# Gated cross attention with a routed expert layer: least and greatest of the last group read from the rows before normalization, routing choices of the first batches two steps earlier

## The reference

```python
x = x + tanh(g_xattn) * attention(layernorm(x), ctx)      # 16 heads of 16, rotary, causal, keys from ctx
xf = layernorm(x)                                          # (3584, 256)
stats = [mean, std, min, max, l2, share of |xf| < 1e-6]    # 6 per token
h = gelu(concat(xf, stats) @ r1_w.T + r1_b)                # 128 hidden
probs = softmax(h @ r2_w.T)                                # 32 experts, top 2 per token
# each expert keeps its 140 best tokens; expert and adapter outputs are added back
x = x + tanh(g_ffn) * out
```

## Time and profile before

| what | us |
|---|---|
| median of 3 runs | 772.27 |
| the runs | 772.27, 768.41, 773.79 |
| the profiled execution | 769.41 |
| its span, first to last instruction | 767.6 |
| busy TensorE, VectorE, ScalarE, GpSimd | 672.7, 526.5, 405.5, 322.6 |
| mean granted TensorE clock | 0.947 |

### The profile page before, as it was taken

The page is one execution under the profiler, slowest core; times in us unless marked ns, Lnnn a source line. Parts: engine busy times, 40 slices in busy tenths (PEclk is TensorE's granted clock), DMA queues, the critical chain, the costliest instruction groups (busy, mean ns, idle before and its releaser), DMA issues.

```text
span 767.6 us, 17452 instructions
## 1 busy us (share of the span) xinstructions
PE 672.7 (88%) x5247; PEld 528.0 (69%) x5247; DVE 526.5 (69%) x1548; ACT 405.5 (53%) x1569; POOL 322.6 (42%) x339
## 2 busy tenths in 40 slices
PE   8799999999999999999888212699999999999992
PEld 4466666666666566666655101399999999999992
DVE  6764786767867678675899888776665676445441
ACT  2367777877778777787683565022222222222220
POOL 3443462444624446244112000436566565665633
PEclk9999999999999999999999655799999999999996
DMA  5600020200202002010001601159898999889921
GB/s 167 221 31 25 26 61 14 73 27 25 63 10 72 26 25 70 3 48 1 26 26 49 223 1 23 35 165 260 250 275 235 267 263 269 261 243 262 278 30 15
DMA packets 57723, 85.28 MB, mean 111 GB/s; under 512 B 11442, under 2 KB 28464, under 8 KB 57648
## 3 DMA queue, kind: packets, MB, share of 16 engines
q1 hardware_dynamic: 47456, 73.77, 29.4%
q0 software_dynamic: 9216, 9.76, 8.1%
q10 hardware_dynamic: 976, 0.89, 0.5%
HBM read 71.70 MB, written 12.69 MB: 110 GB/s over the span
## 4 chain that ended last, share of the span: by engine, by line
PE 54%; ACT 18%; DVE 16%; issue 7%; DMA 2%; POOL 1%; ACTq 1%; DVEq 0%; POOLq 0%
PE pair L991 19%; PE bank L1001 10%; ACT arena L1298 8%; DVE arena L1470 5%; PE pair L1623 5%; PE bank L1586 3%; PE pair L1632 2%; PE bank L1651 2%; ACT arena L561 2%; PE pair L1618 2%; ACT arena L1246 2%; PE bank L1013 2%; ACT arena L1286 1%; PE bank L1565 1%; DMA rows_out<-arena,slot_row 1%
## 5 line engine op out<-in xcount | busy, mean ns | idle before, releaser
L1298 ACT ACTIVATE arena<-pair,arena 112x112 f32<-112x112 f32 x512 | 175.5, 365 | 63.1 <-DVE arena L1470 58.3
L991 PE MATMUL pair<-arena,we 128*128 128x140 f32 x1024 | 138.2, 283 | 0.6 <-ACT arena L901 0.6
L881 POOL DMA_INDIRECT rows_out<-arena,slot_row x64 | 94.4, 1475 | 95.7 <-DVE arena L932 69.1
L991 PEld LDWEIGHTS pair<-arena,we 128*128 128x128 f32 x1024 | 128.5, 190 | 0.9 <-issue 0.9
L909 ACT ACTIVATE arena<-pair 128x140 f32<-128x140 f32 x160 | 45.8, 287 | 150.1 <-PE pair L991 98.1
L944 DVE SCALAR_TENSOR_TENSOR arena<-arena,pair 128x140 f32<-128x140 f32 x160 | 47.7, 298 | 94.7 <-ACT arena L909 49.0
L1298 ACT ACTIVATION_READ_ACCUMULATOR arena<-pair,arena 112x1 f32 x512 | 109.8, 215 | 0.0
L870 POOL DMA_INDIRECT arena<-rows,slot_row x64 | 62.7, 979 | 86.8 <-issue 86.8
L1001 PE MATMUL bank<-arena,we 128*128 128x140 f32 x512 | 83.4, 286 | 0.0
L1470 DVE TENSOR_REDUCE arena<-pair 112x8 f32<-112x896 f32 x64 | 68.9, 1077 | 18.3 <-PE pair L1623 17.6
L1632 PEld LDWEIGHTS pair<-tab,arena 112*112 112x112 f32 x512 | 51.6, 133 | 30.7 <-issue 28.7
(11 more groups left out here) (209 smaller groups left out, 1197.3 us busy)
## 6 DMA issues: line engine op xcount, KB each, us to landing
we<-w_experts_in SPq DMA_DIRECT2D x192, 256.0 KB
wa<-w_adapters_in SPq DMA_DIRECT2D x16, 384.0 KB
arena<-ctx_in SPq DMA_DIRECT2D x8, 448.0 KB, 4.5
arena<-x_in SPq DMA_DIRECT2D x8, 448.0 KB, 3.8
rows_out<-arena SPq DMA_DIRECT2D x8, 448.0 KB, 3.3
rows<-arena SPq DMA_DIRECT2D x8, 448.0 KB, 3.3
arena<-rows,slot_row POOLq DMA_INDIRECT x64
rows_out<-arena,slot_row POOLq DMA_INDIRECT x64
```

The costliest lines, as they stand in the source:

```text
L881: nc.gpsimd.indirect_dma_start(d["out"], bass.IndirectOffsetOnAxis(ap=slot_row[:, h, e:e + 1], axis=0), yr[e % 2][:, h, :], None, compute_ ...
L991: last = nc.tensor.matmul(banks[m % 4][:, part * CAP:(part + 1) * CAP], w[:, col0:col0 + 128], xet[j % 2][:, c, :], start=(c == 0), stop=( ...
L1298: last = nc.scalar.activation(pr[s % 2][:, j, :], banks[BS[s % 4]][0:T, j * T:(j + 1) * T], ACT.Exp, bias=nmx[s // 2 % 2][:, s % 2, j:j + ...
```

## The change

Four edits, all in pass 7 and the tail.

1. In the tail, the least and the greatest value of each row are taken from the rows before normalization (`extremes`, two reductions over three batches in step 4 and two over the last batch in step 6), and then normalized with the row's mean and reciprocal deviation (`normalize_extremes`, two small operations in step 12). The two reductions over all four batches of normalized rows in steps 10 and 12 go. `extremes` also waits until the statistics of group 6 have been read.
2. Logits, shifts, exponentials and choices of the batches of sets 0 and 1 stand earlier, most by two steps. Set 2 keeps its shift and its choices in place.
3. `IDLE` goes from 24, 7 and 2 to 28, 4 and 2 products.
4. `SETUP` goes from step 2 to step 3.

```diff
-IDLE = {7: 24, 12: 7, 14: 2}
+IDLE = {7: 28, 12: 4, 14: 2}
...
-LOGITS = {1: (0, 1), 3: (2, 3), 7: (4, 5), 20: (6,)}
+LOGITS = {0: (0, 1), 1: (2, 3), 5: (4, 5), 20: (6,)}
 EARLY_ROWS = (slice(0, 16), slice(16, 24), slice(24, 28))
-SHIFTED, RAISED = (3, 7, 22), (4, 8, 22)
+SHIFTED, RAISED = (1, 5, 22), (2, 6, 22)
 PARTS = 9
-CHOOSE = {5: ((0, 0), (0, 1)), 7: ((0, 2),), 9: ((0, 3), (0, 4)), 13: ((0, 5),), 15: ((0, 6), (1, 0), (1, 1)),
-          16: ((0, 7), (0, 8)), 18: ((1, 2),), 19: ((1, 3),), 20: ((1, 4),), 22: ((1, 5), (1, 6)),
-          29: ((1, 7), (1, 8)), 30: tuple((2, part) for part in range(PARTS))}
+CHOOSE = {3: ((0, 0), (0, 1)), 5: ((0, 2),), 7: ((0, 3), (0, 4)), 9: ((0, 5),), 11: ((0, 6),), 12: ((0, 7),),
+          13: ((0, 8), (1, 0)), 14: ((1, 1),), 15: ((1, 2),), 16: ((1, 3), (1, 4)), 18: ((1, 5),),
+          19: ((1, 6),), 22: ((1, 7), (1, 8)), 30: tuple((2, part) for part in range(PARTS))}
...
-SETUP = 2
+SETUP = 3
...
+        def extremes(par, some):
+
+            dve.wait_ge(s_xft, 3 * (NG - 1))
+            for i, op in ((2, ALU.min), (3, ALU.max)):
+                last = nc.vector.tensor_reduce(st[:, some, i], x1[par][:, some, :], X, op)
+            link(last)
+
+        def normalize_extremes():
+            ends = st[:, :, 2:4]
+            link(nc.vector.tensor_tensor(ends, ends, mv2[:, :, 0:1].to_broadcast([T, GB, 2]), ALU.subtract))
+            link(nc.vector.tensor_tensor(ends, ends, rs2.unsqueeze(2).to_broadcast([T, GB, 2]), ALU.mult))
+            dve.sem_inc(s_mv3, 1)
...
                         if j == GB - 1:
                             residual_stats(g - back, (par + back) % 2, j)
+                            if not own:
+                                extremes((par + back) % 2, slice(j, GB))
                 if prev and s == LN2_STATS:
                     residual_stats(g - 1, 1 - par, GB - 2)
+                    if not own:
+                        extremes(1 - par, slice(0, GB - 1))
...
                 for part in XF_STATS.get(s, ()) if prev else ():
-                    xf_stats(g - 1, part)
+                    if own or part in ("mean", "zeros"):
+                        xf_stats(g - 1, part)
+                    elif part == "max":
+                        normalize_extremes()
```

## The result

| | us |
|---|---|
| before, median (768.41 to 775.67) | 773.03 |
| changed, median (779.55 to 784.33) | 782.60 |
| ratio | 1.0134, interval 1.0096 to 1.0171 |
| profiled execution of the changed kernel, its span | 783.96, 782.1 |

The change makes the kernel 1.34% slower, by the ratio some 10.4 us (7.4 to 13.2). The two profiled executions lie further apart than that, with 14.5 us of span between them: the one of before was among its fastest, the one of the changed kernel the second slowest of four. 3.1 of the 14.5 us lie ahead of pass 7, in code that is the same in both (the first maximum reduction of the whole program starts at 26.2 us instead of 24.2). No run shows where they come from, and they are not counted as the change's. From the first reduction of pass 7 to the first operation of the search it is 83.8 us instead of 71.8, and from there to the end 0.5 us less than before.

What follows compares the result with a forecast made beforehand. In pass 7 the ring over the engines or VectorE's queue sets each distance. Pass 7 +5.8, up to the normalization +1.8, behind it -0.7: +6.9 us on 771.0 gives 777.9, likeliest 775 to 780.5, 8 in 10 within 769 to 784.

Steps and rivals of the forecast that it cites:

- Logits in steps 0 and 1: Pass 7, first distance: a second logits product ahead of the causal mask delays the scores of step 2; +2.1 us.
- Steps 2 to 4: Pass 7: VectorE's queue holds setup and two parts of set 0 for setup and shift, 5.5 us as before; +0.
- Steps 4 to 6: Pass 7: VectorE waits for set 1's logits behind the output projection, 7.3 us where 5.10 stood; +2.2 us.
- Steps 6 to 10: Pass 7: shift and its wait leave step 7 and an exponential has moved; -1.1 and -0.4 us.
- Steps 10 to 14: Pass 7: VectorE's queue sets both distances and gets more parts of the choices; +1.6 and +1.4 us.
- Step 14 to the product: End of pass 7: ScalarE and the chain over the engines take 4.9 us, smaller VectorE load saves nothing; +0.
- Tail up to the normalization: New reductions delay the last batch's residual by 1.5 us, and VectorE's later queue is 0.3 longer; normalization +1.8 us.
- Behind it: Tail behind the normalization: four unread products instead of seven free TensorE sooner for turning the statistics; -0.7 us.
- The clock in the hidden rows of the tail: TensorE's clock falls there as before, 0; -1.3 us if it stays high, +1.0 if it falls sooner.
- rival C: Pass 7: with longer pauses TensorE's clock falls there too; +4 us more, 782; chance 0.12.
- Rival A: Pass 7: the logits cost TensorE nothing that matters, scores of step 2 on time; +3.4 us, 774.4; chance 0.17.
- rival B: Pass 7 and tail: VectorE's idle time is the whole bound, moved work fills it; 2.9 us faster, 768.1; chance 0.14.

Runs made afterwards that it cites:

- warm_pass_2: Changed kernel plus unread products in TensorE's pauses of steps 3, 7 and 15 of pass 7, the last ahead of turning the sums: 778.45, ratio 1.0096.
- one_product_less: Changed kernel with the logits product of step 0 left out, so the first eight batches are routed by what the bank held: 782.70 for one execution.
- late_choices_warm: late_choices with the unread products of warm_pass_2 added: 778.97, ratio 1.0103.
- no_extremes: Changed kernel with least and greatest values taken from the normalized rows again, as before the change: 778.43, ratio 1.0076.
- idle_only: Kernel before with four unread products in place of seven behind the hidden rows of the tail: 769.53, ratio 0.9969.
- extremes_only: Kernel before with the new reductions ahead of the normalization alone: 775.64, ratio 1.0040.
- setup_first: Kernel before with four unread products for seven, setup in step 1, logits of batches 8 to 23 one step earlier: 770.07, ratio 0.9969.
- late_choices: Changed kernel with the choices from part 6 of set 0 on back in their steps of before: 786.40, ratio 1.0167.
- warm_pass: Changed kernel plus unread products in steps 3, 7 and 15 of pass 7, those of step 15 behind the pause: 780.40, ratio 1.0105.
- late_choices_again: The unchanged kernel of late_choices profiled once more; second profiled executions of it and the changed kernel took 780.98 and 782.76.

## Why the prediction was right

The forecast was 777.9 in a range of 769 to 784, and the measured 782.6 lies in it, on the side forecast. It lies in the upper part, which the prediction gave 0.28. Of the 4.7 us between them, 2.0 are the base: the forecast set its sum on 771.0, and the median of before came out at 773.03. What is left is, by the runs above, mainly the clock. In differences, +6.9 was foretold and +10.4 measured by the ratio, +12.0 between the distances of the two profiles. Point by point, against warm_pass_2, which has the schedule of the change at full clock in pass 7:

- Logits in steps 0 and 1: foretold +2.1, measured +2.0 (5.70 to 7.70). The product ahead of the mask is shown as its cause by one_product_less.
- Steps 2 to 4: 0 foretold, +0.25.
- Steps 4 to 6: +2.2 foretold, +1.6 at full clock (6.70), +3.2 in the changed kernel. VectorE does wait for the logits product, as foretold, but at full clock its shift starts 3.9 us behind the reduction, not 4.5.
- Steps 6 to 10: -1.1 and -0.4 foretold; -0.75 and -0.3.
- Steps 10 to 14: +1.6 and +1.4 foretold; +1.25 and +1.5. The sum of the pass: +5.8 foretold, +5.55 measured.
- Step 14 to the product: 0 foretold, +0.02, though part 6 had gone from there. So it had cost nothing in step 15, which is how the sum takes it (the words beside it, that it hadn't been free, say the opposite). late_choices_warm shows how far this carries: putting it and the parts behind it back saves 3.2 us in the pass and gives back 2.6 in the tail and behind it. So the cover in the pass was real but for the 0.6 us by which P grew, and it was worth little to the kernel.
- Tail up to the normalization: +1.8 foretold, +1.74 measured (Q unchanged, N 5.98 to 7.72).
- Behind it: -0.7 foretold, -0.83 and -0.75 measured in the two profiles of the changed kernel, whose statistics were turned right behind the four products as foretold. In warm_pass_2 it was -0.10, since the clock took the turning of the rows along, a case that the prediction had priced at +1.0.
- The clock in the hidden rows of the tail: low as foretold (3.19 and 3.26 us), and the four more products did not keep it up. In no_extremes, where next to no pause followed the 28 products, the rows took 1.77 us, but in idle_only they did so too, behind the pause of 1.30 us, so the pause alone doesn't decide it.

The step that was mis-sized is the clock. I had it as rival C with a chance of 0.12 and a price of 4 us, and the sum otherwise had it fall in the tail only, at no cost. In both profiles of the changed kernel it fell in pass 7 as well. The sums differ from warm_pass_2 by 4.8 and 6.0 us; the times by 3 to 4. The two terms belong together: the schedule makes the kernel 7.2 us slower by the sum of warm_pass_2 (7.4 by its ratio, 5.0 to 9.7), for which 6.9 was foretold, and the clock adds about what C says, which gives 10.9 for the 10.4 measured. That the range held 782.6 is owed to the share that C had in it, not to the forecast.

That the longer pauses bring the clock down is shown as far as this: the four profiles with the pass of before or nearly so (before, extremes_only, idle_only, setup_first) have no fall in it, all six with the early logits and nothing filled have one to four (in late_choices the only one is that at the first logits product), and filling three of the pauses kept the clock up in both profiled kernels that had them filled ahead of the sums. warm_pass, which left the third pause open, had its fall just there. Against a fixed rule stand one_product_less, with no fall behind its pause of 1.59 us, and a pause of 1.57 us in step 12, which warm_pass_2 left open and had no fall behind. It isn't shown for the fall at the first logits product, which comes ahead of the pauses filled. The three profiles with products in steps 3 and 7 were free of it, and so were three of the six without, which leaves chance open.

Rival A fell with the first distance of 7.70 and with one_product_less, rival B with the reading that VectorE's pause stayed and a second one came. One figure beside B is wrong: with 3.5 us added and 0.7 taken off, the time would turn at 2.8 us of idle time filled, not at 4.2. The forecast doesn't use it. Its likeliest range of +3.9 to +9.4 is not the plain sum of its bounds either, which give +0.9 and +9.2; the measured difference lies above both upper ends.

## What to carry to other kernels

A pause of one engine isn't room if what would fill it waits for an engine that is full at that moment; fill it with work that has its inputs already, as the setup in setup_first. In a chain over three engines with written orders, look at the distance between two turns of the ring and name for each distance whether the ring or one queue sets it: with that, the seven distances here were foretold to 0.6 us each at full clock. Where a schedule gives TensorE new pauses, price the low clock with it, and if you fill them with unread products, put these ahead of what TensorE waits for, not behind. Here that won 3 of the 10 us back, and the schedule without new pauses was still the faster one.

## What the runs showed of the hardware

The clock can stay low while TensorE is busy by the profile. In late_choices TensorE was busy for 30.00 of 30.00 us from 372 to 402 us, and the granted clock was 0.50 throughout. In late_choices_again, the same program, it was 0.83 on average in the same stretch, with 26.15 us busy, so the low state is in part what fills the time: the same work takes longer. The fall at 361.1 us in late_choices came when TensorE had last paused for 0.23 us, at 357.3 us. The three falls in the first profile of the changed kernel came behind pauses of 1.59, 2.64 and 1.23 us. The Trainium skill, "TensorE: Matmul & The Clock Gate", section "What's actually happening", has activity release the throttle; by busy time, the trace of late_choices does not agree: from 361 to 402 us it was busy for 41.00 of 41.00 us at 0.50. What the chip takes for activity was not tested.
